# Where the first probability transposes of a step stand: in front of its 24 score products, or between their halves

## The chip, the cores and the metric

The kernel runs on one core of a Trainium2 chip. The metric is the device time of one execution in microseconds (us). The time before is 2560.58 us, the median of three runs (2560.01 to 2562.6).

## The reference

One pre-norm transformer layer over 8 batches of 2048 rows with 256 features, in 32-bit floating point:

```
def attn(X, W_Q, W_K, W_V):
    Q = xpos(X @ W_Q); K = xpos(X @ W_K, downscale=True); V = X @ W_V
    p = softmax(einsum('bqd,bkd->bqk', Q, K), axis=-1)
    p = p * (0.9 ** abs(n - m))[None]          # decay with the distance
    return einsum('bqk,bkv->bqv', p, V)
def ffn(x, w_gate, w_up, w_down):              # each operand of a product is first
    gate = fp4_linear(x, w_gate); y = fp4_linear(x, w_up)   # rounded to FP4, in blocks of 16
    return fp4_linear(silu(gate) * y, w_down)  # 256 -> 704 -> 256
x = x + attn(layernorm(x), W_Q, W_K, W_V)
x = x + ffn(layernorm(x), w_gate, w_up, w_down)
```

## The kernel before

A first stage (some 320 us) normalises the rows, makes queries, keys and values of all batches and puts them into device memory. Everything after it is one pipeline over 8 x 16 = 128 steps. Step `s` of a batch works on several tiles of 128 rows at once, each at another stage: the scores of tile `s`, attention (probabilities times values) of tile `s-1`, the gate and up products of tile `s-2`, and the down product of tile `s-5` (`LAG`). The first batch is written out (`first_plan`), the seven others are a loop whose body has 16 steps, and five end steps follow.

Every product is computed from operands split into an upper and a lower part, with three of the four part products (`product`, L482), so scores of one tile are 24 matmuls of 512 columns: 12 for the first half of the 2048 keys, 12 for the second. Each half goes to two banks of the tile `score`. VectorE takes the maximum of each half (`maxima`, L1197), ScalarE the exponentials into `probs` (`exponentials`, L785), and GpSimd (POOL) multiplies them by the decay, group by group (`decays`, L944), counting in the semaphore `decayed`. The decay is exactly zero farther than 7 blocks of 128 keys away, so attention of a tile takes 8 to 15 blocks, in groups of at most 4 (`groups`, L73); the first group is the odd one, 1 to 4 blocks.

A group of probabilities is transposed by TensorE into one bank of a ring of three (`group`, L585). ScalarE copies the upper part out of it (`upper`, L759), VectorE the lower part (`lower`, L1187), which frees the bank; then TensorE multiplies with the values (`attend`, L599). The first two groups of tile `s-1` are transposed by `attend_begun` (L594), the others during `attend`. The ring's order is fixed by `plan_slots` (L81): in a step the first two groups, the transposed row tile `xqT`, the other groups and the transposes `hT`, and at the end the three pieces of the gate/up product. A bank can be taken when the use three places before is over (`slot`, L540). So the first group needs the bank that the first gate/up piece of the step before had, and the second group that of the second piece. Those are freed by VectorE in `h_made` (L1279, the instruction of L1285), in the middle of other work.

Every engine does its work in the order in which it is written, one after the other:
- TensorE (`step`, L668): scores of `s` with the first two groups of `s-1` between the halves; attend `s-1` with the transposes of `xqT` and `hT`; gate/up of `s-2`; down of `s-5`.
- VectorE (`step`, L1313): maximum of the first half; lower parts of the first two groups; maximum of the second half and the row's negative maximum; the other lower parts; rounding of `h` (L1035 to L1042); the residual; scales with the three `h_made` pieces in between; rounding of `x`; and at last `result` (L1308), which adds the down product.
- ScalarE (L827): queries of `s+1`, upper parts, exponentials of `s`, gate.
- GpSimd (L991): lower part of the queries of `s+1`, decays of `s`, roundings.
- SyncE issues the DMAs (L443): in step `s` the query tile `s+2`, in the last step of a batch the next batch's keys (`load_keys`, L415, which waits for the score half that last reads them), values, edges, the store of tile `s-5` (after `result`) and the residual of tile `s`.

Of the kernel before, what the change touches and what calls it, by code (L numbers as in the profile page):

```python
# [124 lines left out]
def build(nc, X, WQ, WK, WV, WG, WU, WD, rot_tab, decay_tab, eye, out):  # L125
# [5 lines left out]
    with ExitStack() as ctx:  # L131
# [114 lines left out]
        def later(j):  # L246
            return j, NS0 + (j - 1) * NS, loop_plan
# [11 lines left out]
        def has(at, t):  # L259
            return t < T and (t >= 0 or at[2] is not first_plan)  # L260
# [9 lines left out]
        def tile(at, t):  # L270

            return at[0] * T + t
# [208 lines left out]
        def _(pe):  # L481
            def product(dst, stat, mov, ks, ends=True):  # L482

                n = len(ks) * len(PASSES)
                i = 0
                for k in ks:
                    for a, m in PASSES:
                        mm = pe.matmul(dst, stat(a, k), mov(m, k), start=i == 0, stop=ends and i == n - 1)  # L488
                        i += 1
                return mm  # L490
# [56 lines left out]

            def scores(at, s):
                g = tile(at, s)
                pe.wait_ge(q_split, g + 1)  # L550
                for o in range(4):
                    if s == 0 and at[2] is not first_plan:
                        pe.wait_ge(k_back[o], at[0] * 32)
                    if s == 0 and at[2] is first_plan:
                        pe.wait_ge(k_split, (B - 1) * NC + o + 1 + PRIME)
                        if o % 2 == 0:
                            pe.wait_ge(rotated, 2 * NCH - 1 + o // 2 + PRIME)
                    elif s == 1 and at[2] is first_plan:
                        if o % 2 == 0:
                            pe.wait_ge(exped, 2 * g - 1 + o // 2)  # L560
                    elif o == 0:
                        pe.wait_ge(exped, 2 * g)
                    mm = product(score[:, o, :], lambda a, k: q_st[s % 2][:, a, k, :],
                                 lambda m, k: keys[m][:, k, o * CH:(o + 1) * CH], range(KT))
                    if o % 2:
                        mm.then_inc(scored, 1)
                    if o == 1:
                        attend_begun(at, s - 1)

            def weights(at, i):  # L570
                dst = slot(at, "w", i)
# [13 lines left out]
            def group(at, t, g):  # L585

                pe.wait_ge(decayed, pieces_before(at, t) + g + 1)
                dst = slot(at, "pT", t, g)
                for n, kb in enumerate(groups(t % T)[g]):
                    source = edge_probs[:, int(kb > t % T), :] if (t % T, kb) in CORNERS else probs[:, kb * P:(kb + 1) * P]  # L590
                    mm = pe.transpose(dst[:, n * P:(n + 1) * P], source, ident[:])  # L591
                mm.then_inc(filled, 1)

            def attend_begun(at, t):  # L594
                if has(at, t):
                    group(at, t, 0)
                    group(at, t, 1)
# [70 lines left out]
            def step(at, s):  # L668
                if s < T:
                    scores(at, s)  # L670
                else:
                    attend_begun(at, s - 1)
                if s == 0 and at[2] is first_plan:
                    pe.wait_ge(v_split, 2 * NC)
                for i in weights_at(at, s):
                    weights(at, i)
                attend(at, s - 1, lambda: x_transposed(at, s - 2), lambda h: h_transposed(at, s - LAG, h))
                gate_up(at, s - 2)
                down(at, s - LAG)
# [3 lines left out]
            with nc.Fori(1, B, engines=bass.OrderedEngineSet([pe.engine]), hint_back_edge=True) as j:  # L683
                at = later(j)
# [703 lines left out]
```

## Time and profile before

| | |
|---|---|
| Median of three runs | 2560.58 us |
| Profiled execution, its own time | 2561.61 us |
| Its span, first to last instruction | 2559.7 us |
| Busy: TensorE, VectorE, GpSimd, ScalarE | 99%, 84%, 71%, 59% of the span |
| Mean granted TensorE clock | 0.997 |

PE is TensorE, PEld its weight loads, DVE VectorE, ACT ScalarE, POOL GpSimd, SP SyncE. A line of a timeline has the start in us, the busy time in us, engine, source line, operation, output and inputs, shapes and count; at its end may stand the idle time before it and what ended that. Instructions of one kind that follow each other are one line. The ends of matmuls are modelled and overlap the next, so distances of starts tell how long something takes.

### The profile page before, as it was taken

How to read it: one execution, taken by the hardware profiler on the slowest of the kernel's cores; microseconds unless marked ns; L12 is line 12 of the kernel's file. 1: busy time of each engine (PE TensorE's matmuls, PEld its weight loads, DVE VectorE, ACT ScalarE, POOL GpSimd, SP SyncE). 2: the span in 40 equal slices, each digit the busy share in tenths (PEclk: the TensorE clock that was granted, in tenths of full speed). 3: DMA queues.
4: the chain of work that ended last, by engine and by line, in shares of the span. 5: the costliest groups of instructions: out<-in, count | busy, mean ns of one | idle time of the engine just before them, and what ended most of it. 6: DMA issues, size and time to landing. Idle time of an engine off the chain costs nothing.

```text
span 2559.7 us, 51974 instructions
## 1 busy us (share of the span) xinstructions
PE 2530.1 (99%) x16188; PEld 2291.1 (90%) x16188; DVE 2144.5 (84%) x4759; ACT 1505.0 (59%) x2966; POOL 1819.3 (71%) x1929
## 2 busy tenths in 40 slices
PE   8999999999999999999999999999999999999997
PEld 7888879999999899999999899989998999999997
DVE  8999878888888888888888888888888888888886
ACT  5766555656555665566556556565556655665654
POOL 6999956667767676667767676667666776677665
PEclk9999999999999999999999999999999999999999
DMA  8878411122111311131112211131113111211110
GB/s 285 301 279 292 179 50 30 34 78 74 40 38 42 108 36 42 34 106 42 42 34 83 69 40 38 42 108 39 41 34 105 41 42 34 90 62 40 38 38 22
DMA packets 163473, 203.27 MB, mean 79 GB/s; under 512 B 15184, under 2 KB 116752, under 8 KB 163216
## 3 DMA queue, kind: packets, MB, share of 16 engines
q1 hardware_dynamic: 163216, 200.01, 24.0%
q8 instruction: 141, 2.31, 0.4%
q14 instruction: 116, 0.95, 0.1%
HBM read 103.42 MB, written 77.59 MB: 71 GB/s over the span
## 4 chain that ended last, share of the span: by engine, by line
PE 81%; DMA 2%; issue 1%; SPq 1%; DVE 1%; ACT 1%; POOL 0%; DVEq 0%; ACTq 0%; POOLq 0%
PE score L488 25%; PE acc L623 19%; PE ring L488 18%; PE acc L488 8%; PE ring L591 6%; PE ring L643 3%; DMA keys<-k_dram 2%; PE ring L582 1%; PE acc L665 1%; SPq L419 1%; ACT probs L791 0%; DVE hT L1189 0%; DVE h_buf L1285 0%; SPq L369 0%; ACT L817 0%
## 5 line engine op out<-in xcount | busy, mean ns | idle before, releaser
L488 PE MATMUL score<-keys,q_st 128*128 128x512 f32 x3072 | 759.4, 396 | 5.1 <-ACT probs L791 2.6
L488 PEld LDWEIGHTS score<-keys,q_st 128*128 128x128 f32 x3072 | 558.7, 188 | 114.6 <-issue 3.0
L623 PE MATMUL acc<-vals,pT 128*128 128x256 f32 x3984 | 556.9, 287 | 0.8 <-DVE pT L1189 0.8
L961 POOL TENSOR_TENSOR probs<-probs,decay 128x512 f32<-128x512 f32 (+3 forms) x416 | 447.0, 1088 | 144.8 <-ACT probs L791 144.8
L488 PE MATMUL ring<-w_gu,xqT 128*128 128x512 f32 (+1 forms) x2304 | 510.3, 375 | 0.0
L623 PEld LDWEIGHTS acc<-vals,pT 128*128 128x128 f32 x3984 | 498.9, 189 | 6.2 <-DVE pT L1189 2.0
L488 PEld LDWEIGHTS ring<-w_gu,xqT 128*128 128x128 f32 x2304 | 419.4, 189 | 63.5
L761 ACT ACTIVATE pT<-ring 128x512 fp32r<-128x512 f32 (+3 forms) x432 | 226.9, 535 | 376.4 <-PE ring L591 368.9
L1202 DVE TENSOR_REDUCE smax<-score 128x1 f32<-128x1024 f32 x256 | 312.1, 1219 | 100.3 <-PE score L488 99.6
L1189 DVE TENSOR_TENSOR pT<-ring,pT 128x512 fp32r<-128x512 f32 (+3 forms) x432 | 250.5, 604 | 69.1 <-ACT pT L761 67.9
L967 POOL TENSOR_TENSOR xv<-xv,xe 128x256 f32<-128x256 f32 x128 | 94.3, 737 | 270.4 <-DVE xv L1042 270.4
L761 ACT ACTIVATE xqT<-ring 128x256 fp32r<-128x256 f32 x128 | 49.2, 385 | 401.8 <-PE ring L582 401.8
L791 ACT ACTIVATE probs<-score,nmax 128x1024 f32<-128x1024 f32 x256 | 282.7, 1116 | 2.1 <-DVE nmax L1205 2.0
L488 PE MATMUL acc<-w_dn,hT 128*128 128x256 f32 x1920 | 239.3, 277 | 4.7 <-DVE hT L1189 4.7
L488 PEld LDWEIGHTS acc<-w_dn,hT 128*128 128x128 f32 x1920 | 236.0, 188 | 5.5 <-DVE hT L1189 5.5
L956 POOL TENSOR_TENSOR edge_probs<-probs,decay 128x128 f32<-128x128 f32 x144 | 68.7, 477 | 230.6 <-ACT probs L791 230.6
L982 POOL TENSOR_TENSOR h_buf<-h_buf 128x704 f32<-128x704 f32 x128 | 218.8, 1709 | 4.3 <-DVE h_buf L1042 4.3
L1285 DVE TENSOR_TENSOR h_buf<-h_buf,ring 128x256 f32<-128x256 f32 (+1 forms) x384 | 144.3, 376 | 76.9 <-ACT h_buf L817 76.7
L761 ACT ACTIVATE hT<-ring 128x512 fp32r<-128x512 f32 (+1 forms) x256 | 125.0, 490 | 124.3 <-PE ring L643 124.3
L1189 DVE TENSOR_TENSOR hT<-ring,hT 128x512 fp32r<-128x512 f32 (+1 forms) x256 | 141.2, 553 | 66.4 <-ACT hT L761 66.4
L591 PE MATMUL ring<-ident,probs 128*128 128x128 f32 x1328 | 194.8, 273 | 0.0
L488 PE MATMUL score<-xT,w_in 128*128 128x512 f32 x768 | 188.3, 394 | 2.3 <-DVE xT L1070 2.3
(132 smaller groups left out, 4610.4 us busy)
## 6 DMA issues: line engine op xcount, KB each, us to landing
k_dram<-keys SPq DMA_DIRECT2D x56, 512.0 KB, 4.6
keys<-k_dram SPq DMA_DIRECT2D x56, 512.0 KB, 7.8
edge<-vals SPq DMA_DIRECT2D x288, 64.0 KB, 2.0
q_raw<-q_dram SPq DMA_DIRECT2D x129, 128.0 KB, 2.6
x_in<-X SPq DMA_DIRECT2D x32, 512.0 KB, 4.6
q_dram<-q_stage SPq DMA_DIRECT2D x32, 512.0 KB, 5.6
x_res<-X SPq DMA_DIRECT2D x128, 128.0 KB, 2.1
out<-x_res SPq DMA_DIRECT2D x128, 128.0 KB, 1.7
```

The costliest lines, as they stand in the source:

```text
L488: mm = pe.matmul(dst, stat(a, k), mov(m, k), start=i == 0, stop=ends and i == n - 1)
L591: mm = pe.transpose(dst[:, n * P:(n + 1) * P], source, ident[:])
L623: mm = pe.matmul(pv_out, pT[g % 2][:, a, j * P:(j + 1) * P], edge[place][:] if kb in edges else vals[m][:, kb, :], start=i == 0, stop=i == ...
L643: mm = pe.transpose(dst[:, j * P:(j + 1) * P], hq[t % 2][:, k * P:(k + 1) * P], ident[:])
L761: act.activation(dst, src, ACT.Copy).then_inc(hi_done, 1)
L791: act.activation(probs[:, h * 2 * CH:(h + 1) * 2 * CH].rearrange("p (j n) -> p j n", j=2), score[:, 2 * h:2 * h + 2, :], ACT.Exp, bias=nma ...
L961: op = pool.tensor_tensor(probs[:, k0:k1], probs[:, k0:k1], decay[:, off + k0:off + k1], ALU.mult)
L967: pool.tensor_tensor(xv[:], xv[:], xe[:], ALU.subtract).then_inc(x_levelled, 1)
L982: pool.tensor_tensor(hv[t % 2], hv[t % 2], he[t % 2], ALU.subtract).then_inc(h_levelled, 1)
L1189: dve.tensor_tensor(dst, src, hi.bitcast(F32), ALU.subtract).then_inc(freed, 1)
L1202: dve.tensor_reduce(smax[:, h:h + 1], score[:, 2 * h:2 * h + 2, :], AX.XY, ALU.max).then_inc(maxed, 1)
L1285: dve.tensor_tensor(hv[t % 2][:, p0:p0 + w], silu[t % 2][:, p0:p0 + w], bank(at, "gu", t, p)[:, w:2 * w], ALU.mult).then_inc(freed, 1)
```

## The change

The call of `attend_begun` moves from the middle of the scores' loop to in front of it. It is in front of the wait for the split queries, too.

```
             def scores(at, s):
                 g = tile(at, s)
+                attend_begun(at, s - 1)
                 pe.wait_ge(q_split, g + 1)
                 for o in range(4):
                     ...
                     mm = product(score[:, o, :], lambda a, k: q_st[s % 2][:, a, k, :],
                                  lambda m, k: keys[m][:, k, o * CH:(o + 1) * CH], range(KT))
                     if o % 2:
                         mm.then_inc(scored, 1)
-                    if o == 1:
-                        attend_begun(at, s - 1)
```

No other engine's program changes, and no instruction is added or removed.

## Rows read from the trace of the kernel before

**Rows 1.** The page's busy table, and its chain that ended last, by engine.
```profile
PE 2530.1 (99%) x16188; PEld 2291.1 (90%) x16188; DVE 2144.5 (84%) x4759; ACT 1505.0 (59%) x2966; POOL 1819.3 (71%) x1929
...
PE 81%; DMA 2%; issue 1%; SPq 1%; DVE 1%; ACT 1%; POOL 0%; DVEq 0%; ACTq 0%; POOLq 0%
```

**Rows 2.** Waits of the whole trace: who, for whom; us in total, times, longest.
```profile
PEld score L488 <- DMA keys<-k_dram: 2.9, 4, 1.0
```

**Rows 3.** Timeline of TensorE, steps 1 and 2 of the fifth batch.
```profile
1427.85 0.71 PE L591 MATMUL ring<-ident,probs 128*128 128x128 f32 x5
1428.31 3.02 PE L488 MATMUL score<-keys,q_st 128*128 128x512 f32 x12
...
1440.57 0.39 PE L665 MATMUL acc<-w_dn,hT 128*128 128x256 f32 x2
1440.80 2.91 PE L488 MATMUL score<-keys,q_st 128*128 128x512 f32 x12
```

**Rows 4.** Timeline of TensorE: first and last six products of a first half.
```profile
1425.10 1.55 PE L488 MATMUL score<-keys,q_st 128*128 128x512 f32 x6
...
1426.49 1.52 PE L488 MATMUL score<-keys,q_st 128*128 128x512 f32 x6
```

**Rows 5.** Timelines of POOL and VectorE ahead of the step at 1440.80.
```profile
1436.97 1.94 POOL L961 TENSOR_TENSOR probs<-probs,decay 128x128 f32<-128x128 f32 x2 [1.50 <-ACT probs L791]
...
1440.20 0.41 DVE L1285 TENSOR_TENSOR h_buf<-h_buf,ring 128x256 f32<-128x256 f32 x1
```

**Rows 6.** Timelines of TensorE and VectorE, a step with 8 moved transposes.
```profile
659.64 2.92 PE L488 MATMUL score<-keys,q_st 128*128 128x512 f32 x12
...
662.63 1.21 DVE L1202 TENSOR_REDUCE smax<-score 128x1 f32<-128x1024 f32 x1
663.76 1.28 DVE L1189 TENSOR_TENSOR pT<-ring,pT 128x512 fp32r<-128x512 f32 x2
666.20 1.23 DVE L1202 TENSOR_REDUCE smax<-score 128x1 f32<-128x1024 f32 x1 [1.16 <-PE score L488]
```

**Rows 7.** Timelines of POOL and weight loads: a release and its start.
```profile
311.75 0.74 POOL L909 TENSOR_TENSOR q_st<-q_raw,q_st 128x256 fp32r<-128x256 f32 x1
...
312.55 1.46 PEld L488 LDWEIGHTS score<-keys,q_st 128*128 128x128 f32 x7 [0.21 <-POOL q_st L909]
```

**Rows 8.** First batch, step 1: timelines; window: busy of PE, PEld, DVE, ACT, POOL, clock, DMA.
```profile
323.43 4.49 PE L488 MATMUL score<-keys,q_st 128*128 128x512 f32 x12 [2.24 <-ACT probs L791]
...
331.16 0.49 PE L574 MATMUL ring<-ident,hq_buf 128*128 128x128 f32 x3
...
324.52 1.70 POOL L961 TENSOR_TENSOR probs<-probs,decay 128x256 f32<-128x256 f32 x2 [3.59 <-ACT probs L791]
...
324.60:327.90 3.30, 3.30 (x9) 2.41 (x9) 1.94 (x6) 1.95 (x8) 3.30 (x5) 0.50 0.42 116
```

**Rows 9.** First batch, step 2: timelines of TensorE and POOL.
```profile
339.30 2.99 PE L488 MATMUL score<-keys,q_st 128*128 128x512 f32 x12 [0.34 <-ACT probs L791]
...
345.89 0.62 PE L623 MATMUL acc<-vals,pT 128*128 128x256 f32 x3 [0.28 <-DVE pT L1189]
...
339.23 1.71 POOL L961 TENSOR_TENSOR probs<-probs,decay 128x128 f32<-128x128 f32 x2 [11.21 <-ACT probs L791]
```

**Rows 10.** First batch, step 5: timelines of TensorE and VectorE.
```profile
383.06 2.93 PE L488 MATMUL score<-keys,q_st 128*128 128x512 f32 x12
...
379.53 1.86 DVE L1042 SCALAR_TENSOR_TENSOR h_buf<-h_buf 128x704 f32<-128x704 f32 x1
...
382.78 0.42 DVE L1285 TENSOR_TENSOR h_buf<-h_buf,ring 128x256 f32<-128x256 f32 x1
...
383.58 0.41 DVE L1285 TENSOR_TENSOR h_buf<-h_buf,ring 128x256 f32<-128x256 f32 x1
```

**Rows 11.** Windows near the end of the kernel, columns as in rows 8.
```profile
2533.00:2536.30 3.30, 2.41 (x10) 2.20 (x11) 0.62 (x2) 1.21 (x3) 3.01 (x5) 0.50 0.12 40
2536.50:2539.70 3.20, 3.20 (x9) 2.43 (x9) 1.66 (x4) 1.11 (x1) 2.10 (x2) 0.50 0.03 5
```

**Rows 12.** Timelines of VectorE and SP, last step of the second batch.
```profile
841.93 1.21 DVE L1202 TENSOR_REDUCE smax<-score 128x1 f32<-128x1024 f32 x1
...
844.11 6.09 SPq L419 DMA_DIRECT2D keys<-k_dram  x8
```

More of the change, by code:

```diff
@@ L549, in scores @@
                 g = tile(at, s)
+                attend_begun(at, s - 1)
                 pe.wait_ge(q_split, g + 1)
@@ L566, in scores @@
                         mm.then_inc(scored, 1)
-                    if o == 1:
-                        attend_begun(at, s - 1)
             def weights(at, i):
```

## The prediction

> **What bounds the kernel now.** I read the page's busy table and its chain of waits first [rows 1]. TensorE is busy for 2530.1 of 2559.7 us, and 81% of the chain that ended last is its own instructions. A busy TensorE is not yet a full one, so the wait list came next. It shows who holds TensorE up: in the whole trace the loads of keys cost its weight loads 2.9 us in four waits [rows 2], and the other entries for TensorE are of the same few microseconds each. The timeline of a later batch shows what that means [rows 3]: down products to 1440.8, 12 score products from 1440.80, 5 transposes in a block whose 12 following score products start at 1428.31 in the step before, and no idle figure anywhere. From 1425.10 to 1440.80 is one step, 15.7 us, with no hole. So work that only changes its place on TensorE costs nothing, unless it arrives at its new place before what it waits for. The question is what the first two transposes' groups wait for, and how late that is, when they stand about 2.75 us earlier (1425.10 to 1427.85).
>
> **What is removed and added.** No instruction is removed or added. For 127 of 128 steps 5 to 8 transposes go from behind 12 score products to in front of them. They wait for two things. POOL has to have weighted the first and second group of probabilities by the decay. And VectorE has to have freed the ring banks: the first group takes the bank of the gate/up product's first piece, the second that of its second piece, of the same step.
>
> **Later batches, 112 steps.** In the step shown, POOL ends both decay products at 1436.97 + 1.94 = 1438.91, and the block would start when the score products start now, at 1440.80 (weight load 0.11 us before) [rows 3, 5]. That is 1.8 us of cover. Over all later steps I found 1.6 to 2.6 us for the second group: 0 cost. VectorE frees the second piece's bank at 1440.20 + 0.41 = 1440.61 [rows 5]. This step has one transpose in the first group, so the second group's weight load would come at 1440.69 + 0.11 = 1440.80. From the end of a releasing instruction to the weight load that it lets go are 0.06 us (311.75 + 0.74 to 312.55) [rows 7]. So 0.12 us of cover is left, and this is the tightest step of a batch (step 2, seven times); step 1 has 0.30, all others 0.4 or more. I take 0 and keep the slip as a rival.
>
> The first half of the scores ends 0.55 to 0.87 us later, the second at the same time. VectorE's maximum of the first half and its two lower-part copies move with it where VectorE is not late by itself. The worst case is 8 transposes [rows 6]: step start 659.64, maximum at 662.63 (2.99 behind), copies to 663.76 + 1.28 = 665.04, then 1.16 us of idling to the second maximum at 666.20. Moved by at most 0.87 the copies end at 665.9: 0.3 us of the 1.16 are left, and the second maximum, the row's negative and the exponentials stay. The first attend product needs only the first copy, 0.6 us earlier: hidden too. Without that idle time each 0.1 us over would be paid once a step.
>
> The SP queue: the loads of the next batch's keys wait for the first half of the last step's scores, which is now 0.55 us later. But VectorE already reduces that half at 841.93, while SP issues the first of the 8 loads at 844.11 [rows 12], because it comes from a store, a residual load and a query load, in order, and the store hangs on VectorE. 844.1 - 841.9 = 2.2 us cover 0.55: nothing, else at most 0.55 x 7 = 3.9 us. ScalarE copies the transposes' upper parts in time it idles through now.
>
> **First batch.** There the pipeline is still filling and the cover isn't there.
> Step 1 [rows 8]: TensorE ends 11 transposes of weights, idles 2.24 us and starts scores at 323.43, as soon as half the exponentials are there. The probabilities' decay ends at 325.25 and 326.22 (two instructions from 324.52 to 326.22, of which the first takes about 0.73). With the change, 2 transposes at 325.3, 3 at 326.3; TensorE is granted 0.50 of its clock (1.2 GHz) from 324.6 to 327.9, after that idling, so they are over at about 327.0, and 2.3 score products at 0.427 us fit until 328.0. The 21.7 left take 0.2285 each: 332.95, against 331.16 now. Cost: 1.8 us.
> Step 2 [rows 9]: scores start at 339.30; decay of the second group ends at 339.23 + 1.71 = 340.94. Four transposes from 341.08, scores from 341.5, 24 x 0.2285 = 5.5: attend at 347.0 against 345.89. Cost: 1.1.
> Step 5 [rows 10]: VectorE, late, frees the two pieces at 383.20 and 383.99; scores start at 383.06 now. First group 383.3 to 383.8, second 384.1 to 384.6, attend at 390.1 instead of 383.06 + 6.4 = 389.46. Cost: 0.6.
> Steps 3 and 4 just pass. What stands behind each wait is the whole step, so all of it counts: 1.8 + 1.1 + 0.6 = 3.5.
> **The low clock of step 1.** Such a stretch comes at two lengths. At the end of the kernel one went on from 2533.0 to 2539.7 [rows 11], twice as long as the one of step 1; there TensorE idled on into the stretch and then had transposes. With the change step 1 is like that (idle to 325.3, 5 transposes, a hole between). A second stretch of 3.4 us holds 3.4 / 0.427 = 8 score products where 15 would have run: 7 x 0.2285 = 1.6 us. Ends: 0 and 1.6; I take 1.6, by the nearer row.
>
> **What comes back.** The first six score products behind the down product take 1.55 us, the last six of the same twelve 1.52 [rows 4]: a new kind of product runs in a little slower. Now scores start twice a step, behind the down product and behind the transposes; with the change once. 0.03 x 127 = 3.8 us less. The rows are rounded to 0.01, and transposes behind a down product are not in the trace of the loop: ends 0.05 x 127 = -6.4 and, should they run in worse, 0.01 x 127 = +1.3. I take -3.8, the measured one.
> The page "TensorE: Matmul & The Clock Gate" of the Trainium skill (Back-to-back issue gap) has the distance of two products as columns over clock plus a fixed 2.5 ns, whatever stood in front. By that rule nothing comes back; the trace does not agree in size (1.52 us over six is above it) nor in being fixed (1.55 against 1.52).
>
> **Sum.** 3.5 + 1.6 - 3.8 = +1.3 us. The profiled execution took 2561.61 us, its span 2559.7 and 1.9 around it; it is 1.0 over the median 2560.58 of the three runs. As a difference it goes on the median: 2561.9.
>
> **Rivals.**
> (a) The low clock of step 1 lasts 3.4 us as now: 3.5 - 3.8 = -0.3, 2560.3. For it: TensorE is full from 326.3 on.
> (b) Nothing comes back: 3.5 + 1.6 = +5.1, 2565.7. The two starts differ by only 0.03 us; this also is the page's rule.
> (c) Slower, through one wait: in step 2, and from there step 1, of the seven later batches the second group waits for the gate/up piece. It decides once VectorE is 0.12 us later there. In step 5 of the first batch VectorE's rounding took 1.86 us (379.53) [rows 10] and the bank came 0.7 us too late; so late seven times is 4.9, with (b)'s half way back: +1.3 + 4.9 = +6.2, 2566.8. Against it: VectorE's instructions between the second maximum and this piece do not move.
> (d) Faster: run-in saves 0.05 a step and the low clock stays short: 3.5 - 6.4 = -2.9, 2557.7; only with boundary waits for keys [rows 2] gone too, 2.9 more, it passes -5.1. Nothing in the change starts the loads earlier.
> (e) The transposes don't start first, since TensorE's sequencer still tests the scores' conditions in front: 0, 2560.6.
>
> **How the numbers follow.** Forecast 0.47, (a) 0.20, (b) 0.15, (c) 0.10, (d) 0.06, (e) 0.02. A measurement of this kernel can't tell less than 0.2%, 5.1 us, from no change: 2555.5 to 2565.7. Half of (b) and nearly all of (c) lie above it: slower 0.17. Of (d) 0.04 lies below: faster 0.04. The same: 0.79. Range: (d)'s 2557.7 to between (b) and (c), 2557.5 to 2566.0.
>
> **What would show it.** In the changed profile: TensorE idle before the transposes of step 1 about 4.1 us instead of 2.24 before its scores, with a low clock to 331.4 (the 1.6) or 328; 1.4 us before the transposes of step 2; 0.2 and 0.3 before those of step 5. In later batches no idle before any transpose, and steps of 15.66 instead of 15.69 us. VectorE's idle time before the second maximum of an 8-transpose step down from 1.16 to some 0.3, SP's key loads at their old distance. Wrong it is if step 1 or 2 of a later batch is longer, or if a step keeps its length to 0.01 us.

## The result, and the profile after

The changed kernel takes 2565.53 us (median of 22 runs, 2563.97 to 2570.04), the kernel before 2562.16 (22 runs beside them, 2558.86 to 2568.7). The ratio is 1.0014 with a 95% interval of 1.0008 to 1.002, so 3.6 us more (2.0 to 5.1): slower, by an amount that lies inside 0.2%. Forecast were +1.3 us and "the same", in a range whose upper end, 2566.0, is 0.5 us above the time. Of all executions in this document three, of 4237, 4239 and 9022 us, were far longer than the others of their kernels and are left out of every median and ratio.

The page's busy table and its chain hardly differ from [rows 1]; only ScalarE is 13 us less busy. The chain has one point of DMA less.
```profile
PE 2530.8 (99%) x16188; PEld 2299.2 (90%) x16188; DVE 2148.2 (84%) x4759; ACT 1492.0 (58%) x2966; POOL 1817.0 (71%) x1929
...
PE 81%; DMA 1%; issue 1%; DVE 1%; POOL 1%; SPq 1%; ACT 1%; DVEq 0%; ACTq 0%; POOLq 0%
```
The wait list (who waits for whom: us in total, times, longest) shows the new entry: the transposes wait, as the view has it for the decay, three times, and one of the waits is 5 us long. The wait for keys is as small as in [rows 2].
```profile
PEld ring L590 <- POOL probs L960: 7.3, 3, 5.2
...
PE ring L590 <- POOL probs L960: 6.7, 3, 5.0
...
PEld score L488 <- DMA keys<-k_dram: 2.5, 6, 0.7
```
TensorE's timeline of the first batch, steps 1 and 2 (start, us, then the line; idle time before it in brackets), against [rows 8, 9]. Lines past L549 have numbers lower by one than before.
```profile
319.52 1.36 PE L573 MATMUL ring<-ident,gate_in 128*128 128x128 f32 x11
325.89 1.53 PE L590 MATMUL ring<-ident,probs 128*128 128x128 f32 x5 [5.01 <-POOL probs L960]
327.08 8.09 PE L488 MATMUL score<-keys,q_st 128*128 128x512 f32 x24
335.00 1.36 PE L573 MATMUL ring<-ident,hq_buf 128*128 128x128 f32 x11
...
344.81 0.65 PE L590 MATMUL ring<-ident,probs 128*128 128x128 f32 x4 [0.89 <-POOL probs L960]
345.22 7.32 PE L488 MATMUL score<-keys,q_st 128*128 128x512 f32 x24
352.38 0.52 PE L622 MATMUL acc<-vals,pT 128*128 128x256 f32 x3
```
The name of the decay is right for the two waits of step 2. In step 1 the last thing to come was the ring's bank. POOL's first decay product (the first 0.72 us of its two) had ended at 324.94, but of the six copies that VectorE makes out of the ring the second, which frees the first bank, ends at 325.75, and the fourth, which frees the second bank, at 326.41; the weight loads of the two groups start at 325.86 and 326.52.
```profile
324.22 1.68 POOL L960 TENSOR_TENSOR probs<-probs,decay 128x256 f32<-128x256 f32 x2 [3.59 <-ACT probs L790]
...
324.99 1.95 DVE L1193 SCALAR_TENSOR_TENSOR w_gu<-ring,w_gu 128x256 fp32r<-128x256 f32 x6 [3.31 <-ACT w_gu L765]
```
The transposes of weights in step 1 begin at 335.00 instead of 331.16, 3.8 us later, and attention in step 2 at 352.38 instead of 345.89, 6.5 us later. The 24 score products take 8.09 and 7.32 us here, and 5.71 in a later batch. Windows show why (us, busy time of PE, PEld, DVE, ACT, POOL, granted clock, DMA):
```profile
325.30:332.00 6.70, 6.11 (x17) 4.71 (x18) 1.64 (x6) 1.83 (x6) 2.39 (x4) 0.50 0.08 24
332.20:345.00 12.80, 9.79 (x65) 8.03 (x64) 9.75 (x23) 7.45 (x19) 1.92 (x3) 1.00 0.10 26
345.80:349.10 3.30, 3.30 (x9) 2.62 (x8) 2.37 (x5) 0.29 (x1) 1.83 (x3) 0.50 0.02 7
...
2537.20:2540.40 3.20, 2.93 (x11) 2.62 (x12) 1.14 (x3) 1.26 (x3) 3.06 (x4) 0.50 0.11 33
2540.60:2543.00 2.40, 2.40 (x13) 2.03 (x12) 0.85 (x3) 1.49 (x2) 1.59 (x2) 1.00 0.00 0
```
Step 1 has 6.8 us at 1.2 GHz where it had 3.4, and step 2, which had none, has 3.4. The stretch at the kernel's end, 6.8 us in [rows 11], is 3.4 in this execution. Step 5, against [rows 10]:
```profile
389.55 0.63 PE L590 MATMUL ring<-ident,probs 128*128 128x128 f32 x4 [0.17 <-DVE h_buf L1284]
390.34 0.63 PE L590 MATMUL ring<-ident,probs 128*128 128x128 f32 x4 [0.16 <-DVE h_buf L1284]
```
Later batches: TensorE in steps 1 and 2 of the fifth, against [rows 3]. No idle figure, one start of score products per step, and 15.67 us from 1429.42 to 1445.09 where [rows 3, 4] have 15.70 from 1425.10 to 1440.80.
```profile
1429.42 0.71 PE L590 MATMUL ring<-ident,probs 128*128 128x128 f32 x5
1429.89 5.71 PE L488 MATMUL score<-keys,q_st 128*128 128x512 f32 x24
1435.43 0.87 PE L622 MATMUL acc<-vals,pT 128*128 128x256 f32 x6
...
1445.09 0.71 PE L590 MATMUL ring<-ident,probs 128*128 128x128 f32 x5
```
VectorE in the step with 8 moved transposes, against [rows 6]:
```profile
669.87 1.23 DVE L1201 TENSOR_REDUCE smax<-score 128x1 f32<-128x1024 f32 x1 [0.74 <-PE score L488]
671.01 1.28 DVE L1188 TENSOR_TENSOR pT<-ring,pT 128x512 fp32r<-128x512 f32 x2
672.59 1.23 DVE L1201 TENSOR_REDUCE smax<-score 128x1 f32<-128x1024 f32 x1 [0.30 <-PE score L488]
```
Laid side by side, the starts of one tile's gate/up product in both traces tell where the time is (after minus before, us):
```
exponentials of step 0 (ScalarE)      -0.3
tile 0   (first batch, its step 2)    +6.2
tile 3   (first batch, its step 5)    +6.8
tile 13  (end of the first batch)     +6.5
tile 125 (end of the last batch)      +3.5
end of the span                       +2.4
```
All of the loss is there by step 5 of 128. The trace of after comes 0.3 us early out of the first stage, which the change does not touch, so the first two steps cost 0.3 more than the table has. From step 5 on the loss shrinks: 0.35 to 0.49 us per later batch over its steps 1 to 15 (mean 0.40, or 0.027 a step), and 0.24 in sum at the seven starts of a batch, where the wait for keys varies by -0.66 to +0.75 with how the loads land. The last 1.1 us go with the shorter low clock at the end, which this execution happened to have: the medians differ by 3.4, not by 2.4.

### The profile page after: what moved, and what is told of

The parts are those of the page before. It is cut to its first block, busy times and chain, and to the rows that moved or that the text cites. A ratio compares the mean times of both kernels' runs of the same rounds, so it can differ in the third digit from the quotient of the medians.

```text
span 2562.1 us, 51974 instructions
## 1 busy us (share of the span) xinstructions
PE 2530.8 (99%) x16188; PEld 2299.2 (90%) x16188; DVE 2148.2 (84%) x4759; ACT 1492.0 (58%) x2966; POOL 1817.0 (71%) x1929
## 4 chain that ended last, share of the span: by engine, by line
PE 81%; DMA 1%; issue 1%; DVE 1%; POOL 1%; SPq 1%; ACT 1%; DVEq 0%; ACTq 0%; POOLq 0%
PE score L488 25%; PE acc L622 19%; PE ring L488 18%; PE acc L488 8%; PE ring L590 6%; PE ring L642 3%; PE acc L664 1%; PE ring L581 1%; DMA keys<-k_dram 1%; SPq L419 1%; DMA edge<-vals 0%; ACT probs L790 0%; POOL h_buf L981 0%; POOL h_buf L975 0%; POOL hq_buf L988 0%
## 5 line engine op out<-in xcount | busy, mean ns | idle before, releaser
L488 PE MATMUL score<-keys,q_st 128*128 128x512 f32 x3072 | 737.8, 396 | 1.8 <-DVE keys L1095 1.4
L488 PEld LDWEIGHTS score<-keys,q_st 128*128 128x128 f32 x3072 | 569.5, 189 | 119.4 <-DMA keys<-k_dram 2.5
L760 ACT ACTIVATE pT<-ring 128x512 fp32r<-128x512 f32 (+3 forms) x432 | 220.1, 531 | 71.4 <-PE ring L590 63.9
```

What stands on the lines that cost most here:

```text
L760: act.activation(dst, src, ACT.Copy).then_inc(hi_done, 1)
```

## The experiments

The account to be tested: all cost lies in steps 1, 2 and 5 of the first batch, about half of it is the halved clock after the waits, and the loop gives back some 0.03 us a step since score products start once instead of twice. The rivals: the loop costs too or gives nothing back; the gain comes from elsewhere (the place of VectorE's work, not TensorE's starts); what was seen in the first batch is chance.

**One part each.** The new order in the seven later batches alone:
```diff
-    attend_begun(at, s - 1)                      # in front of the scores
+    front = at[2] is not first_plan
+    if front: attend_begun(at, s - 1)
...
+        if o == 1 and not front: attend_begun(at, s - 1)
```


> The first two groups of transposes stand in front of the scores in the seven later batches only; the first batch keeps its old order. Theory A (all that the change costs is paid in steps 1, 2 and 5 of the first batch, 6.9 us in the trace, and every later step gives back about 0.027 us, since the score products start once instead of twice): 112 x 0.027 = 3.0 us less than before, no idle time of TensorE in front of a transpose of the loop. Rival B (the loss is in the loop, through waits that a single trace doesn't show): 3 to 4 us more than before. Rival C (nothing comes back in the loop, the shorter steps of the trace are chance): within 0.5 us of before.

2558.14 us (11 runs; 2561.55 for the kernel before, 31 runs), ratio 0.9989 (0.998 to 0.9999). In its trace every later batch is 0.35 to 0.48 us shorter over steps 1 to 15, 2.8 us in sum. So the loop's half of the change is a gain of the size forecast. A single trace need not show it whole: the seven starts of a batch, where it hangs on the landing of keys, give 0.65 us back in this one, and in the other kernels with the new loop they come to between -1.0 and +5.3 against before. And the first batch, where its code is that of before, has no low clock in step 1 at all:
```profile
323.20 3.01 PE L488 MATMUL score<-keys,q_st 128*128 128x512 f32 x12 [2.23 <-ACT probs L794]
...
324.60:327.90 3.30, 3.11 (x17) 2.38 (x16) 2.84 (x7) 2.60 (x9) 3.22 (x5) 1.00 0.35 102
```
Before, the same 12 products behind the same idling (2.24) took 4.49 us [rows 8]. The kernels below that keep the old order in step 1 and fill nothing divide: three have the low clock there, two have not. This part of the clock is chance. Both traces with the new order in all of the first batch and nothing filled, that of the change and the next one, have 6.8 us of low clock in step 1 and some 3.4 in step 2.

The other part alone, `front = at[2] is first_plan`:

> The transposes stand in front in the first batch only; the loop keeps its old order. Theory A: 6.9 us of waits and low clock in steps 1, 2 and 5, less 15 x 0.027 = 0.4: 6.5 us more than before. Rival B: within 1 us of before, since later slack takes the first batch's waits up. Rival C: 6.9 us more, which these rounds can't tell from A.

2568.97 us (11 runs), ratio 1.0026 (1.0017 to 1.0035): +6.7. Its trace is at +5.4 at tile 0's step 2, +5.9 at tile 3, +5.8 at tile 125, and its later batches move by 0.15 us or less. The two parts, -2.8 and +6.7 by their ratios, make +3.9, and the whole is +3.6.

**Is the cost only in steps 1, 2 and 5?** `front = not (at[2] is first_plan and s in (1, 2, 5))`:

> The transposes stand in front in all steps but 1, 2 and 5 of the first batch. Theory A: no new wait is left, 124 x 0.027 = 3.3 us less than before, and the fastest of all. Rival B: about as slow as the change, 3 to 4 us more. Rival C: as before.

2558.47 us (11 runs), ratio 0.9986 (0.9977 to 0.9995). It removes the loss, as it should. The 0.3 us by which it should beat the loop alone are less than the two intervals tell apart. Its trace has a new loss of 1.3 us in step 5. TensorE, POOL and VectorE there:
```profile
389.12 1.68 PE L626 MATMUL acc<-vals,pT 128*128 128x256 f32 x12 [1.06 <-DVE pT L1192]
...
377.79 2.86 POOL L964 TENSOR_TENSOR probs<-probs,decay 128x512 f32<-128x512 f32 x2 [0.21 <-ACT probs L794]
...
378.00 1.50 DVE L1041 TENSOR_SCALAR h_buf<-h_buf 128x704 f32<-128x704 f32 x1
379.53 1.86 DVE L1045 SCALAR_TENSOR_TENSOR h_buf<-h_buf 128x704 f32<-128x704 f32 x1
```
Two of VectorE's rounding instructions took 1.50 and 1.86 us beside POOL's two decay products; in the changed kernel the median of the first kind is 0.527 and of the second 0.893 over 128 tiles. The 1.86 stands in every trace, before the change too [rows 10]; the 1.50 is new. VectorE is 1.5 us behind, and TensorE waits 1.06 us for its copy. To see whether the old order in step 5 brings this about, one more kernel keeps it in steps 1 and 2 only:

> The transposes in front in all steps but 1 and 2 of the first batch; one look at step 5 of the first batch. Theory A (VectorE frees the gate/up banks late there, 0.66 us as in the change): idle time in front of the transposes of step 5, and no later wait of step 5 for VectorE. Rival H (VectorE's delay in step 5 is fixed by GpSimd and only shows at another place; with the old order in step 5 it cost 1.06 us in front of attend): 1.0 us or more in front of the transposes of step 5.

One execution: 2559.26 us. Step 5 has the two waits of the change (0.20 and 0.16 us), costs 0.68 as there, and has no wait at 389:
```profile
382.22 0.63 PE L594 MATMUL ring<-ident,probs 128*128 128x128 f32 x4 [0.20 <-DVE h_buf L1288]
383.01 0.63 PE L594 MATMUL ring<-ident,probs 128*128 128x128 f32 x4 [0.16 <-DVE h_buf L1288]
```
So the waits of step 5 are the order's (0.7 us). The 1.06 is not the old order's: the loop-only kernel has the old order in that step too, and not the wait. The traces show where it begins, one step earlier, at a small instruction of VectorE next to a decay product of POOL. First the kernel with the wait, then the loop-only kernel:
```profile
366.66 1.08 DVE L1262 TENSOR_SCALAR xs<-xam,rstd 128x16 f32<-128x16 f32 x1
366.70 1.01 POOL L964 TENSOR_TENSOR probs<-probs,decay 128x384 f32<-128x384 f32 x1
...
366.76 0.23 DVE L1262 TENSOR_SCALAR xs<-xam,rstd 128x16 f32<-128x16 f32 x1
366.82 1.04 POOL L964 TENSOR_TENSOR probs<-probs,decay 128x384 f32<-128x384 f32 x1
```
Started 0.04 us ahead of POOL it took 1.08 us and ended with POOL's product (367.74 and 367.71); started 0.06 us ahead it took 0.23. Late by this, VectorE lets POOL go on 0.5 us later, waits 0.67 us for POOL in turn, and starts the instruction of 0.53 us behind POOL's start (378.00, 377.79) instead of ahead of it. The kernel at the end of this section, which has the old order in the whole first batch, shows the same chain (1.07, 0.62, 1.51 and a wait of 1.05). Some hundredths of a microsecond decide it, not the order; how often it happens over executions isn't known.

**What gives time back in the loop?** If it is the number of starts of score products, then two starts behind transposes a step (three in all) must cost time. In the loop, group 0 after 6 score products and group 1 after 18:
```diff
-        if o == 1: attend_begun(at, s - 1)
+        if at[2] is first_plan:
+            if o == 1: attend_begun(at, s - 1)
+        elif o in (0, 2) and has(at, s - 1): group(at, s - 1, o // 2)
```


> In the loop the first group of transposes stands behind the first six score products and the second group behind the first eighteen, so score products start three times a step instead of twice; the first batch keeps its old order. Theory A: one more start of about 0.027 us in 112 steps, 3.0 us more than before. Rival C (the distance of two products doesn't depend on what stood in front): as before. If VectorE's second maximum comes later by the second group's copies, it has at least 1.8 us until ScalarE asks for it, so nothing of that shows.

2563.76 us (11 runs), ratio 1.0007 (0.9997 to 1.0016). The times alone settle nothing; the trace does: each later batch is 0.23 to 0.35 us longer over steps 1 to 15, where the change is 0.40 shorter. That is 0.021 us a step for one start more and -0.027 for one less, 2.2 us in sum instead of the 3.0 expected; the interval of the times holds both.

Group 0 in front and group 1 between the halves leaves one break in the scores, but moves half of the work to the new place:

> In the loop the first group of transposes stands in front of the scores and the second between their halves; the first batch keeps its old order. Theory A (what comes back is one start of the score products less): they start twice a step, as before, so within 0.5 us of before. Rival G (what comes back is that the first group's copies are made earlier): at least half of the 3.0 us of the loop come back.

2562.83 us against 2562.22 (11 runs), ratio 1.0003 (0.9994 to 1.0013); the trace has +0.17 to +0.33 a batch (0.017 a step). Two starts of scores, and nothing comes back, although the first group stands where the change puts it. The rival by which the gain is the place of the transposes falls, as far as the first group goes. But the count of starts doesn't explain the small loss: it is two, as before. The single steps say more. Laid beside before, step by step over six later batches, most differences of the changed kernel repeat to 0.003 us, and they are not alike: -0.086 us in step 6 and -0.054 in step 7, but -0.007, +0.005 and 0.000 in steps 10, 12 and 13 and -0.001 in step 4. By the number of transposes moved the means are -0.046 (5 transposes, five steps), -0.029 (6, four steps) and -0.01 (7 and 8, six steps). So -0.027 is a mean of unequal steps, and not the price of one start; the loop-only kernel and the kernel with 29 filling products below show the same ones. What sets it in a step no run here shows.

**How near is the next wait?** In the loop the first two groups one place earlier still, ahead of the down product of the step before:
```diff
     gate_up(...)
+    if at[2] is loop_plan and 1 <= s < T - 1: attend_begun(at, s)
     down(...)
```


> In steps 2 to 15 of the later batches the two groups stand one place earlier still, in front of the down product (1.94 us) of the step before; steps 0 and 1 have them in front of the scores and the first batch has its old order. It measures how much cover the new place has left. Theory A, from the trace of before: the second gate/up piece's bank would come 0.5 to 1.8 us too late in each step (1.94 less the 0.2 to 1.5 by which it is early now), 15 us a batch, 106 us in all, with VectorE named in front of the transposes. Rival F (VectorE frees the banks earlier when the transposes come earlier, since the order adapts): under 20 us.

One execution: 2653.68 us, 13.6 us more per batch over steps 1 to 15 (0.45 to 1.73 a step). The wait list and one step's timeline:
```profile
PEld ring L594 <- DVE h_buf L1290: 107.8, 196, 1.3
...
1497.15 0.66 PE L594 MATMUL ring<-ident,probs 128*128 128x128 f32 x4 [0.28 <-DVE h_buf L1290]
```
The wait is the one that rival (c) named, VectorE freeing the bank of the gate/up piece. At the change's place it costs nothing; one place earlier, ahead of the 17 down products (1.94 us), some 0.9 us a step.

**How much of the first batch's cost is the clock?** TensorE is given products to do while it would wait, and the order stays as changed. The first attempt wrote them into the very bank that the transposes are to use (20 in front of the first group of step 1, 1 of the second, 4 and 3 in step 2):

> The change, and in steps 1 and 2 of the first batch TensorE fills its waits with 28 score-like matmuls of 512 columns (21 in step 1, 7 in step 2) into the ring banks, which the transposes then overwrite. Theory A (of the change's 6.2 us in these two steps only 2.1 are waits, the rest is the granted clock of 0.50 that follows them, 10.2 us long in the trace): no low clock between 320 and 350 us, 4.2 us less than the change, so about 1 us less than before. Rival D (the waits themselves cost it, the clock is a side effect): as the change, 3 to 4 us more than before.

> The transposes stand in front in the seven later batches only, and in step 1 of the first batch TensorE fills its old wait of 2.24 us with 9 matmuls of 512 columns into a ring bank. Theory A: 3.0 us back in the loop, and 1.7 us where step 1's low clock of 3.4 us was (4.49 us for twelve score products instead of 2.75), which the kernel before doesn't meet in every run: 3.0 to 4.7 us less than before. Rival C: 0 to 1.7 less.

Both missed. The first took 2569.28 us (8 runs), ratio 1.0025 (1.0015 to 1.0036); the second, which is the loop-only kernel with 9 such products, 2564.27 (11 runs), ratio 1.0006 (0.9997 to 1.0015). In the second the 9 products idled until 325.98 as well, 4.91 us instead of 2.24. TensorE in the first:
```profile
325.80 7.17 PE L551 MATMUL ring<-keys 128*128 128x512 f32 x20 [4.89 <-DVE w_gu L1203]
```
The bank was not free. It held a piece of the transposed weights until VectorE had copied it, at about 325.7. The products idled as long as the transposes had, and then stood in their way. A failure as a test of the clock, it shows the condition that the prediction names in general and leaves out in step 1: there the first group waits for its bank, which comes 0.8 us after its decay.

The second attempt writes into the bank `acc`, which is free in step 1, and in step 2 into the ring's, free by then:
```diff
+    if s == 1: busy(acc.rearrange("p a d -> p (a d)"), 22); attend_begun(at, 0)
+    elif s == 2:
+        for i, n in enumerate((4, 3)):
+            busy(slot(at, "pT", 1, i)[:, 0:CH], n); group(at, 1, i)
+    else: attend_begun(at, s - 1)
```
where `busy` is n products of 512 columns whose result nobody reads.

> As the kernel with 28 filling matmuls, but the 22 of step 1 write to the bank of the attention sums, which is free then, and so start right behind the transposes of the weights instead of waiting for a ring bank (in the last run they waited for VectorE until 325.8 us and ran 7.2 us beyond, at the low clock). Theory A: TensorE busy from 321 to 326 us, no low clock in steps 1 and 2, the last score product of step 2 at 347.9 us (352.15 in the change): 4.2 us less than the change, about 1 us less than before. Rival D (the clock is a side effect, the waits cost it): as the change, 3 to 4 us more than before.

2561.79 us against 2561.57 (11 and 23 runs), ratio 1.0002 (0.9994 to 1.0011): 29 products more, and less than the change by 3.1 us, each taken against the kernel before beside it (3.7 by the bare medians). The timeline, and windows where the clock of the change was 0.50 (the second where that work stands here):
```profile
320.42 5.28 PE L551 MATMUL acc<-keys 128*128 128x512 f32 x22
...
326.30 0.52 PE L603 MATMUL ring<-ident,probs 128*128 128x128 f32 x3 [0.25 <-DVE w_gu L1206]
326.57 5.74 PE L488 MATMUL score<-keys,q_st 128*128 128x512 f32 x24
...
347.94 0.52 PE L635 MATMUL acc<-vals,pT 128*128 128x256 f32 x3
```
```profile
328.00:332.00 4.00, 4.00 (x19) 3.27 (x19) 2.02 (x3) 0.00 (x0) 0.00 (x0) 1.00 0.00 0
340.00:346.00 6.00, 5.79 (x28) 4.34 (x27) 5.02 (x13) 2.00 (x7) 4.23 (x7) 1.00 0.24 68
```
At full clock the 24 products take 5.74 us instead of 8.09, and attention of step 2 begins at 347.94 instead of 352.38, 4.4 us earlier. The traces leave the first stage at different times, though. VectorE's first maximum starts at 319.39 in the kernel before, at 319.09 in the change, at 318.85 here and at 319.17 in the loop-only kernel. From that maximum on, attention of step 2 is 6.8 us late in the change and 2.6 here, so the low clock of the change cost 4.2. The trace of before has a low clock of its own in step 1 [rows 8], worth 1.2 us: so much earlier, by the same count, is the loop-only kernel, which had none, by tile 0. The waits as such are thus 2.6 + 1.2 = 3.8, and the clock adds 4.2 - 1.2 = 3.0 to what it cost before.

The granted clock averaged over executions says about the same without a trace. It is 0.9964 for the change (22 executions), 0.9979 for the kernel before (31), and 0.9982 for this kernel (11). A difference of 0.0015 in 2560 us is 3.8 us of clock lost.

**The best of it.** The new order in the loop, the old one in the first batch, and 9 products into `acc` where step 1 idles:

> The transposes in front in the seven later batches only, and 9 filling matmuls of 512 columns into the bank of the attention sums in the wait of step 1 of the first batch. Theory A: no low clock around 325 us, 3.0 us back in the loop and up to 1.7 at the start (not in every run of before is the clock low there): 3.0 to 4.7 us less than before. If the start's clock is no matter: 3.0 to 4.0 as with the loop alone.

2556.79 us against 2561.57 (11 and 23 runs), ratio 0.9983 (0.9974 to 0.9991): 4.8 us faster than before by medians and some 8 faster than the change by the two ratios, the best measured here. Its first low clock after the first stage comes at 2515.7. It still has a wait of 1.05 us at 389, like the one above. By how much the 9 products help beyond the order alone, its interval and that of the loop-only kernel don't tell apart.

## Why the prediction was right, and where it was off

"The same" is right, no change beyond 0.2%, and the time lies inside the range. Neither says much for the sum: any amount between -5.1 and +5.1 is "the same", and the time is 0.5 us below the upper end. The amount is +3.4 to +3.6 us instead of +1.3, twice and more. By its steps:

- **What bounds, and no cost in later batches: right.** No transpose of a later batch waits, and none of the steps 1 to 15 is longer by over 0.01 us in the mean of the later batches. Rivals (c) and (e) are out, and so are (a) and (d), by the 6.8 us of low clock in step 1.
- **Run-in, -3.8: size nine tenths of it, the mechanism not borne out step by step.** Measured 0.027 a step in the loop; from tile 3 on, 0.3 us come back in the first batch and 3.0 in the others, the batches' starts included. Rival (b) is out by the loop-only kernel. But one start of 0.03 us less in each step would shorten each alike. Steps 4, 10, 12 and 13 keep their length to 0.01 us, which the prediction names as a sign of being wrong, and steps 6 and 7 give more than it has. That the mean came out near 0.03 was in part luck. The page "TensorE: Matmul & The Clock Gate" of the Trainium skill (Back-to-back issue gap) gives, for a product by itself, columns over clock plus a fixed addition, with no term for what stood in front. By that the loop's order would change nothing, and differences of up to 0.086 us that come again in every later batch say otherwise.
- **Step 1, 1.8 + 1.6 = 3.4: measured 3.8, or 4.1 against the exponentials, which come 0.3 us earlier in this trace.** The stretch of 6.8 us at 1.2 GHz came as taken, to 332.0 instead of 331.4. Missing was the ring bank: the two groups started at 325.9 and 326.5, where the decay of this trace would have let them go at 325.0 and 326.0, after 5.01 us of idling instead of 4.1. Scores start 0.4 us later by this than in the prediction's working.
- **Step 2, 1.1: this is the step that failed.** Measured are 6.5 - 3.8 = 2.65. It was priced as two waits, and they came as priced (0.80 and 0.89 us of idling, in place of 0.34 and 0.28 before). But they too were followed by a low clock, 345.7 to 349.1, which the prediction weighed for step 1 only: 7 products x 0.2285 = 1.6, and 1.1 + 1.6 is what was measured. Nothing in the timeline of before showed a low clock at step 2; yet what the prediction had read for step 1 (idling and transposes, then the clock falls) happened here too, and in the trace with the new order in the first batch alone.
- **Step 5, 0.6: measured 0.66.** The two waits are 0.17 and 0.16.
- **VectorE's idle time before the second maximum: 1.16 to 0.30**, as worked out. **SP's key loads: at their old distance.** The first is issued at 850.28, 6.2 us later than at 844.11 [rows 12], when the step itself is 6.2 later.

Together: 1.3, and 1.6 (clock of step 2), 0.7 (step 1: some 0.4 by the bank, the rest by the later end of its low clock) and 0.5 (less comes back) on top, less 0.3 by which this trace leaves the first stage early, and less 0.3 for a wait on VectorE that the later start takes away between tiles 0 and 3: +3.5. The trace has +3.5 at tile 125, the medians +3.4, the ratio +3.6.

## What to carry to other kernels

An edit in a loop body also edits the prologue that shares its code. Here the body gained 3 us over 112 steps and the first two steps lost 6.8; where a pipeline fills, ask of every moved instruction everything it waits for there, the buffer as well as the data, and keep the old order for those steps. A wait of TensorE can cost twice, once as time and once as what the clock does to the work after it. Ask that of each new wait, not just of the one that already had a low clock before: the waits of 1.7 us in step 2 were followed by 3.4 us at 1.2 GHz, those of 0.3 us in step 5 by none. And a mean over steps that fits a mechanism is no proof of it: read the single steps.

## What the runs showed of the hardware

- The same idling does not always bring the clock down. 2.24 us in front of the scores of step 1 were followed by 3.4 us at 1.2 GHz in the trace of before, 2.23 us in that of the loop-only kernel by none. The page "TensorE: Matmul & The Clock Gate" of the Trainium skill (What's actually happening) has the chip look at activity on a schedule of its own that does not start with the kernel; the two traces agree with that.
- VectorE's rounding instructions, 0.53 and 0.89 us, took 1.50 and 1.86 beside POOL's decay products. Both are 0.97 us longer, less than the decay product each began beside (1.32 and 1.58). The page "SBUF — State Buffer" of the Trainium skill (SBUF: two separate sides) has VectorE and GpSimd take turns at one pair of ports, where the later one waits for the whole of the instruction that runs. The trace agrees in the main: VectorE's 0.53 would have begun at 379.50 - 0.53 = 378.97, and the first of POOL's two ends at 379.11. The small instruction of step 4 agrees closely: it takes 0.23 us in half of the 128 tiles and 0.87 to 1.16 in 46, before and after the change; each of these 46 starts beside a running decay product of POOL and ends 0.03 us behind its end.
- The order of kinds of product changed the length of a step by 0.000 to 0.086 us, in a kernel whose products stand without a gap. With the transposes in front the mean is -0.027; with them behind the first 6 and 18 score products +0.021, in front and in the middle +0.017.
